# ScalarE does exponential, squares of the tile before, then the side eviction, in every step of a language-model tower

## The chip, the cores and the metric

One core of a Trainium2 chip. The metric is the device time of one execution in microseconds, lower is better. Engines: PE does matrix products, VectorE (DVE), ScalarE (ACT) and GpSimd (POOL) do elementwise work, SyncE (SP) issues transfers. Each has its own queue, worked off in order; they meet through semaphores.

## The reference

For 16 sequences of 1024 tokens, three layers are added up:

```
h = tok(x)                      # embedding, 128x128 linear, 6 gated convolutions (3 taps), 128x128 linear
h = h + attn(layernorm(h))      # 4-fold windows gate a mix of two attentions, 8 heads of width 16
h = h + ffn(layernorm(h))       # linear, experts 128 -> 512 -> 128 with gelu, linear, gelu

# in attn, for both attentions a = 1, 2 and every head:
A_a   = softmax(q_a k_a^T * scale)                       # 1024 x 1024
stats = mean, std, max, min of A_a over windows of 4 rows
alpha = sigmoid(mlp(stats of A_1 and A_2))
out   = (alpha * A_1 + (1 - alpha) * A_2) v
```

The standard deviation needs, for each row, the sum of squares of its probabilities. The kernel gets it from exp of twice the shifted score, so that a pass of ScalarE over the scores yields it as the row sum.

## The kernel before, in words

**Units and steps.** One batch is one sequence. It has 16 units (2 attentions x 8 heads), each unit 8 tiles of 128 rows by 1024 keys: 128 steps a batch, 16 batches, 2048 steps, in a loop. The stages of the same batch that come ahead of attention (tokens, convolutions, projections) and behind it (gate, output, experts) are cut into *side tasks*. A planner (`plan`) puts them into the steps ahead of time, `STEP[n]`: those behind attention for the batch before, those ahead of it for the batch after. 95 of the 128 steps have one with a product on PE.

**A step on each engine**, in queue order:

- PE: scores of tile n into one of two slots of `ps_s`; the weighted sum of values for tile n-14 into `ps_o`; the transposed scores of tile n-12 into `ps_t`, which has one slot; then the side product into `ps_w`. All share line L389, so they are told apart by what they write.
- VectorE: `row_max` (L715) copies the negated scores into one of four slots of `neg_s` and gives the row's maximum; `row_min` (L723) reads the tile before; then its side task. In step 8j+5 that is the transposition of a unit's result from `ps_o` to `o_raw` (L731), for which PE's weighted sum of the next step waits.
- ScalarE: `exp_t` (L586) of the transposed scores, from `ps_t` to `exps`; then its side task, mostly the eviction of `ps_w` (L590, L593, L655); then `squares` (L579) of tile n from `neg_s`, with the row sum.
- GpSimd: its own side tasks only: gate of a convolution, layer norms, splitting of queries and keys into bf16 parts (`qk`, which SP then loads for the next unit), splitting of row maxima (`msplit`), from which VectorE makes `mrow`.

**What sets the order.** Scores of tile n wait for the row maximum of tile n-2; transposed scores n wait for exponential n-1; the exponential waits for them. The squares wait for the row maximum of their tile and for an earlier pass of squares; the row maximum of tile n waits for the squares of tile n-4, whose slot it writes. Inside the loop `bank_of` gives the same bank, `ps_w`, to every side product, and `wait_bank` makes each wait until the reader of the one before is done:

```
at = users.index(task) - (1 if phase == "body" else 3)
if at >= 0:
    wait_side(eng, phase, i, READER[users[at][0]], users[at])
```

**Side tasks by name.** `conva`, `convg`: halves of a gated convolution (128x256 to evict); `attw`, `fc1`, `fc2`: the expert stage (`fc1` evicts two pieces of 128x256); `attT`, `nT`, `xnT`, `embT`: four transposes (128x512 to evict); `qk`: a projection of queries or keys, evicted to `stage`; `win`: window means of the statistics. `std`, `gelu1` and `gelu2` need other function tables of ScalarE, so a table load stands before and after them. In steps 64 to 79 `fc1` and convolutions take turns; in 57 to 64 `attw` and convolutions do.

Of the kernel before, what the change touches and what calls it, by code (L numbers as in the profile page):

```python
# [21 lines left out]
ACT = mybir.ActivationFunctionType  # L22
# [4 lines left out]
T = L // P  # L27
# [4 lines left out]
STEPS = U * T  # L32
# [5 lines left out]
RING = 4  # L38
SLOTS_S = 4
# [122 lines left out]
def tower_kernel(nc, ids, table, consts, w_e2h, b_e2h, conv_w, conv_b, w_h2e, b_h2e, wq1, wk1, wq2, wk2, wv, wo,  # L162
                 gw1, gb1, gw2, gb2, gw3, gb3, ln_g, ln_b, attn_w, attn_b, fc1_w, fc1_b, fc2_w, fc2_b,
                 next_w, next_b, out):
    NB = ids.shape[0] - 1

    with ExitStack() as ctx:
        def sb(name, shape, dt=F32):
            return ctx.enter_context(nc.sbuf_tensor(name, shape, dt))

        def sem(name):
            return ctx.enter_context(nc.semaphore(name))
# [32 lines left out]
        neg_s = sb("neg_s", [P, SLOTS_S, L])  # L205
        junk = sb("junk", [P, 2, L], BF16)
# [48 lines left out]
        s_max = sem("s_max")  # L255
        s_min = sem("s_min")
        s_sq = sem("s_sq")
# [14 lines left out]
        def wait_side(eng, phase, i, of, task=None):  # L272

            eng.wait_ge(side_sem[of], side.upto(phase, i, of, task))
# [112 lines left out]
        def _(pe):  # L387
# [53 lines left out]
            def task(phase, i, tk):  # L441
# [40 lines left out]
                elif kind == "attw":  # L482
# [3 lines left out]
                    for q in range(2):  # L486
                        last = mm(bank[:, P * q:P * q + P], x2[:, 2 * c + q, :], ident, start=False,
                                  skip_group_check=True)
                elif kind == "fc1":
                    _, c, j = tk  # L490
                    if (c, j) == (0, 0):
                        pe.wait_ge(s_exw, i * 64 + 64)
# [21 lines left out]
                elif kind in ("conva", "convg"):  # L514
                    _, l, c = tk
                    if l == 0:
                        w("act", ("e2h", min((CH * c + CH) // 512, 1)))
                    else:
                        w("pool", ("convg", l - 1, min(c + 1, NC - 1)))
                    g = kind == "convg"  # L520
                    for k in range(TAPS):
                        last = mm(bank[:, CH * g:CH * g + CH], cw[:, l, k, P * g:P * g + P],
                                  xc[:, l % 2, CH * c + k:CH * c + k + CH], start=(k == 0), stop=(k == TAPS - 1))
                elif kind == "h2e":
                    w("pool", ("convg", LAYERS - 1, NC // 2 * (tk[1] + 1) - 1))
                    for q in range(4):
                        t = 4 * tk[1] + q
                        last = mm(bank[:, P * q:P * q + P], xc[:, 0, 1 + P * t:1 + P * t + P], wh2e[:, :])
                elif kind == "xnT":
                    w("pool", ("ln1",))  # L530
                    last = turn(bank, xn, tk[1])
                elif kind == "qk":
                    _, a, which, k = tk
                    if a == 0:
                        w("act", ("xnT", k))
                    last = mm(bank[:, :], wqk[:, a, which, :], xn_t[:, 512 * k:512 * k + 512])
                elif kind == "v":
                    w("act", ("xnT", tk[1]))
                    for q in range(4):
                        t = 4 * tk[1] + q  # L540
                        last = mm(bank[:, P * q:P * q + P], xn_t[:, P * t:P * t + P], wv_s[:, :])
# [28 lines left out]
        def _(act):  # L570
            def squares(i, n):

                r, t = n // T % RING, n % T
                if t == 0:

                    wait_side(act, "body", i, "pool", ("unit", n // T - 2) if n // T > 1 else None)
                act.wait_ge(s_max, i * STEPS + n + 3)
                act.wait_ge(s_sq, i * STEPS + n + SLOTS_S - 1)
                nc.scalar.activation(junk[:, n % 2, :], neg_s[:, n % SLOTS_S, :], ACT.Exp, scale=-1.0,  # L579
                                     bias=negmax[:, r, t:t + 1],  # L580
                                     accum_out=sumsq[:, r, t:t + 1]).then_inc(s_sq, 1)

            def exp_t(i, n):
                act.wait_ge(s_pv, i * STEPS + n + 1)
                act.wait_ge(s_st, i * STEPS + n + 1)
                nc.scalar.activation(exps[:, n % RING, :], ps_t[:, :, :].rearrange("p c q -> p (c q)"), ACT.Exp,  # L586
                                     scale=0.5).then_inc(s_exp, 1)
# [87 lines left out]
            nc.scalar.activation(g3h[:, :], g3b[:, :], ACT.Copy, scale=0.5)  # L675
            nc.scalar.activation(cb_half[:, :], cb[:, :], ACT.Copy, scale=0.5).then_inc(s_init, 1)
            act.wait_ge(s_init, 4)
            act.sem_inc(s_sq, SLOTS_S)
            act.sem_inc(s_exp, 1)
            act.sem_inc(s_mrow, 64)  # L680
            for tk in PRE:
# [1 line left out]
            with act.Fori(0, NB // E) as group:  # L683
                for e in range(E):
                    i = group * E + e
                    for n in range(STEPS):
                        exp_t(i, n)
                        for tk in STEP[n]:
                            task("body", i, tk)
                        squares(i, n)  # L690
            for n in range(LAG_T):
                exp_t(NB, n)
            for tk in TAIL:
# [389 lines left out]
```

## Time and profile before

| | |
|---|---|
| time, median of 3 runs | 5982.09 us (5976.68 to 5983.98) |
| profiled execution | 5978.36 us, its span 5975.9 us |
| mean granted PE clock | 0.955 of full |
| busy: PE, DVE, ACT, POOL | 87%, 86%, 87%, 41% |
| instructions | 121038 |

A busy share is the time in which an engine has an instruction in work, over the span. The column "idle before, releaser" of a group says how long its engine had stood still ahead of its instructions, and whose work ended that. In the timeline, each line is one instruction or a run of like ones, with its start, its length, its engine and source line, and in brackets the idle time ahead of it.

### The profile page before, as it was taken

The page shows a single profiled execution, that of the slowest core. Times are in us where ns is not written, and L with a number is a line of the kernel's source. Part 1 is how long each engine was busy: PE and PEld are TensorE (multiplying, and loading weights), DVE is VectorE, ACT ScalarE, POOL GpSimd, SP SyncE. Part 2 cuts the span into 40 slices and gives each one's busy share as a digit, 9 for nine tenths or more (in the row PEclk, how much of TensorE's full clock was granted, in tenths as well). Part 3 has the DMA queues.
Part 4 walks back from the last instruction along what each step waited for, and adds up shares of the span by engine and source line. Part 5 has one row for each costly group of instructions (what it writes and reads, how often), then busy time and mean ns, then how long its engine had stood idle before and what let it go on. Part 6 is the DMA issues. An engine that isn't in the chain of part 4 may idle for free.

```text
span 5975.9 us, 121038 instructions
## 1 busy us (share of the span) xinstructions
PE 5203.4 (87%) x34070; PEld 2503.5 (42%) x34070; DVE 5115.8 (86%) x7715; ACT 5221.3 (87%) x7937; POOL 2454.1 (41%) x4439
## 2 busy tenths in 40 slices
PE   6988989889898988989889898988889899898985
PEld 4443434444343443434334343443434344343443
DVE  2989899898998989899898988989899898988982
ACT  2999989899898989989889898989989899898984
POOL 6525344252433525344352433525344352533423
PEclk8999999999999999999999999999999999999997
DMA  1001010010101001010010101001010010101000
GB/s 37 20 23 27 17 31 20 21 27 23 27 19 29 20 21 27 19 31 19 21 28 23 27 19 29 20 21 27 20 31 18 22 28 21 27 20 29 19 22 12
DMA packets 164933, 140.87 MB, mean 24 GB/s; under 512 B 89196, under 2 KB 108268, under 8 KB 164140
## 3 DMA queue, kind: packets, MB, share of 16 engines
q1 hardware_dynamic: 159100, 124.09, 9.0%
q0 software_dynamic: 4352, 8.92, 0.7%
q8 instruction: 291, 4.77, 0.3%
q14 instruction: 374, 3.06, 0.2%
q10 hardware_dynamic: 816, 0.02, 0.0%
HBM read 21.26 MB, written 8.91 MB: 5 GB/s over the span
## 4 chain that ended last, share of the span: by engine, by line
PE 44%; issue 18%; DVE 15%; ACT 11%; POOL 8%; SPq 1%; DMA 1%; DVEq 1%; ACTq 1%; POOLq 1%
PE ps_w L389 19%; PE ps_t L389 10%; PE ps_o L389 9%; DVE neg_s L715 7%; PE ps_s L389 6%; DVE rowmin L723 4%; ACT exps L586 3%; ACT junk L579 3%; DVE bn L735 1%; SPq L330 1%; DVE o_raw L731 1%; POOL part L866 1%; POOL ctmp L986 1%; POOL ctmp L998 1%; ACT hpre L635 1%
## 5 line engine op out<-in xcount | busy, mean ns | idle before, releaser
L715 DVE TENSOR_SCALAR_CACHE_REDUCE neg_s<-ps_s 128x1024 f32<-128x1024 f32 x2048 | 2487.5, 1215 | 599.3 <-PE ps_s L389 526.2
L723 DVE TENSOR_REDUCE rowmin<-neg_s 128x1 f32<-128x1024 f32 x2049 | 2489.5, 1215 | 0.0
L579 ACT ACTIVATE junk<-neg_s,negmax 128x1024 bf16<-128x1024 f32 x2048 | 2353.0, 1149 | 149.4 <-DVE neg_s L715 145.1
L586 ACT ACTIVATE exps<-ps_t 128x1024 f32<-128x1024 f32 x2060 | 2110.6, 1025 | 255.6 <-PE ps_t L389 252.7
L389 PE MATMUL ps_t<-qst,kst 99*128 99x512 bf16 x4120 | 1293.3, 397 | 367.5 <-ACT exps L586 364.1
L389 PE MATMUL ps_o<-exps,v_cur 128*32 128x256 f32 x16512 | 1360.8, 402 | 272.6 <-DVE o_raw L731 240.7
L389 PE MATMUL ps_s<-kst,qst 96*128 96x512 bf16 x4096 | 1260.4, 389 | 44.1 <-DMA kst<-part 35.8
L389 PE MATMUL ps_w<-xc,cw 128*128 128x256 f32 x4704 | 1185.3, 388 | 1.0
L389 PEld LDWEIGHTS ps_w<-xc,cw 128*128 128x128 f32 x4704 | 914.7, 195 | 223.3 <-ACT chan L590 8.9
L389 PEld LDWEIGHTS ps_o<-exps,v_cur 128*32 128x32 f32 x16512 | 330.1, 109 | 1198.1 <-issue 643.9
L866 POOL TENSOR_SCALAR ctmp<-ug 128x256 f32<-128x256 f32 x408 | 165.8, 406 | 1554.7 <-ACT ug L655 1533.0
L389 PEld LDWEIGHTS ps_t<-qst,kst 99*128 99x128 bf16 x4120 | 237.2, 98 | 1289.6 <-ACT exps L586 671.3
L389 PEld LDWEIGHTS ps_s<-kst,qst 96*128 96x128 bf16 x4096 | 399.6, 100 | 456.3 <-issue 162.9
L579 ACT ACTIVATION_READ_ACCUMULATOR junk<-neg_s,negmax 128x1 f32 x2048 | 407.5, 199 | 0.0
L986 POOL TENSOR_TENSOR ctmp<-ctmp,va 128x256 f32<-128x256 f32 x408 | 298.0, 730 | 33.9
L987 POOL TENSOR_TENSOR ctmp<-ctmp,xc 128x256 f32<-128x256 f32 x408 | 279.4, 685 | 32.0
L866 POOL TENSOR_SCALAR mparts<-negmax 128x8 bf16<-128x8 f32 x256 | 52.2, 204 | 580.4 <-DVE neg_s L715 540.5
L590 ACT ACTIVATE va<-ps_w,cb 128x256 f32<-128x256 f32 x392 | 185.5, 473 | 91.0 <-PE ps_w L389 77.7
L655 ACT ACTIVATE ug<-ps_w,cb_half 128x256 f32<-128x256 f32 x392 | 186.4, 475 | 64.6 <-PE ps_w L389 64.0
L866 POOL TENSOR_SCALAR xc<-ctmp 128x256 f32<-128x256 f32 x408 | 167.6, 411 | 67.6 <-POOL ctmp L987 67.6
L866 POOL TENSOR_SCALAR part<-stage 128x512 bf16<-128x512 f32 x132 | 82.1, 622 | 257.8 <-ACT stage L590 243.6
L715 DVE DVE_READ_ACCUMULATOR neg_s<-ps_s 128x1 f32 x2048 | 170.6, 83 | 0.0
(181 smaller groups left out, 4025.1 us busy)
## 6 DMA issues: line engine op xcount, KB each, us to landing
qst<-part SPq DMA_DIRECT2D x1542, 32.0 KB, 2.0
kst<-part SPq DMA_DIRECT2D x1542, 32.0 KB, 2.0
qst<-mrow SPq DMA_DIRECT2D x1028, 1.5 KB
out_dram<-z SPq DMA_DIRECT2D x17, 512.0 KB, 3.2
fc1s<-in_fc_w SPq DMA_DIRECT2D x17, 256.0 KB
fc2s<-in_fc_w SPq DMA_DIRECT2D x17, 256.0 KB
cw<-in_conv_w SPq DMA_DIRECT2D x1, 2304.0 KB
odif<-in_table,idx POOLq DMA_INDIRECT x136
```

The lines of the kernel that those rows point to most:

```text
L330: sp.dma_start(dst[HD * g:HD * g + HD, r, :], part[HD * h:HD * h + HD, a, w, c, :])\
L389: return nc.tensor.matmul(dst, lhs, rhs, start=start, stop=stop, **kw)
L579: nc.scalar.activation(junk[:, n % 2, :], neg_s[:, n % SLOTS_S, :], ACT.Exp, scale=-1.0, bias=negmax[:, r, t:t + 1], accum_out=sumsq[:, r, ...
L586: nc.scalar.activation(exps[:, n % RING, :], ps_t[:, :, :].rearrange("p c q -> p (c q)"), ACT.Exp, scale=0.5).then_inc(s_exp, 1)
L590: return nc.scalar.activation(dst, src, ACT.Identity, **kw)
L635: last = nc.scalar.activation(hpre[:, f, :], hpre[:, f, :], ACT.Gelu)
L655: last = nc.scalar.activation(ug[:, c % 2, :], bank[:, CH:2 * CH], ACT.Tanh, scale=0.5, bias=cb_half[:, 2 * l + 1:2 * l + 2])
L715: nc.vector.tensor_scalar(neg_s[:, n % SLOTS_S, :], ps_s[:, n % 2, :], -1.0, None, ALU.mult, ALU.min, accum_out=negmax[:, r, t:t + 1]).the ...
L723: nc.vector.tensor_reduce(rowmin[:, r, t:t + 1], neg_s[:, m % SLOTS_S, :], axis=AX, op=ALU.max, negate=True).then_inc(s_min, 1)
L866: return nc.gpsimd.tensor_scalar(*args)
L986: chain(i, tt(ctmp[:, 1, :], ctmp[:, 0, :], va[:, c % 2, :], ALU.mult))
L987: chain(i, tt(ctmp[:, 2, :], ctmp[:, 1, :], x_in, ALU.add))
```

## The change

In each step ScalarE does the exponential of tile n, then the squares of tile n-1 (instead of n), then its side task. The squares of the last tile of all are done behind the loop, and the first pass of the loop, for which there is no tile, runs on the zeroed buffer. The counts that are waited for are moved by one with it.

```
 def squares(i, n):
-    r, t = n // T % RING, n % T
+    m = (n - 1) % STEPS
+    r, t = m // T % RING, m % T
     if t == 0:
-        wait_side(act, "body", i, "pool", ("unit", n // T - 2) if n // T > 1 else None)
-    act.wait_ge(s_max, i * STEPS + n + 3)
-    act.wait_ge(s_sq, i * STEPS + n + SLOTS_S - 1)
-    nc.scalar.activation(junk[:, n % 2, :], neg_s[:, n % SLOTS_S, :], ACT.Exp, scale=-1.0,
+        wait_side(act, "body", i, "pool", ("unit", m // T - 2) if m // T > 1 else None)
+    act.wait_ge(s_max, i * STEPS + n + 2)
+    act.wait_ge(s_sq, i * STEPS + n + SLOTS_S - 2)
+    nc.scalar.activation(junk[:, m % 2, :], neg_s[:, m % SLOTS_S, :], ACT.Exp, scale=-1.0,
                          bias=negmax[:, r, t:t + 1],
                          accum_out=sumsq[:, r, t:t + 1]).then_inc(s_sq, 1)
...
-act.sem_inc(s_sq, SLOTS_S)
+act.sem_inc(s_sq, SLOTS_S - 1)
...
     for n in range(STEPS):
         exp_t(i, n)
+        squares(i, n)
         for tk in STEP[n]:
             task("body", i, tk)
-        squares(i, n)
+squares(NB, 0)
```

## Rows read from the trace of the kernel before

**Rows 1.** The page's busy times: engine, busy us, share of the span, instructions.
```profile
PE 5203.4 (87%) x34070; PEld 2503.5 (42%) x34070; DVE 5115.8 (86%) x7715; ACT 5221.3 (87%) x7937; POOL 2454.1 (41%) x4439
```

**Rows 2.** Groups by line: out<-in, shapes, count | busy, mean ns | idle before, releasers.
```profile
L715 DVE TENSOR_SCALAR_CACHE_REDUCE neg_s<-ps_s 128x1024 f32<-128x1024 f32 x2048 | 2487.5, 1215 | 599.3 <-PE ps_s L389 526.2
L579 ACT ACTIVATE junk<-neg_s,negmax 128x1024 bf16<-128x1024 f32 x2048 | 2353.0, 1149 | 149.4 <-DVE neg_s L715 145.1
```

**Rows 3.** Timeline of a convolution step: start us, length, engine, line, what [idle before].
```profile
3126.68 0.60 PE L389 MATMUL ps_t<-qst,kst 99*128 99x512 bf16 x2
3127.12 1.46 PE L389 MATMUL ps_w<-xc,cw 128*128 128x256 f32 x6
3127.38 1.03 ACT L586 ACTIVATE exps<-ps_t 128x1024 f32<-128x1024 f32 x1
...
3128.69 0.47 ACT L590 ACTIVATE va<-ps_w,cb 128x256 f32<-128x256 f32 x1 [0.29 <-PE ps_w L389]
...
3129.51 0.60 PE L389 MATMUL ps_t<-qst,kst 99*128 99x512 bf16 x2
```

**Rows 4.** Timeline of ScalarE in a step without a side task.
```profile
3130.22 1.02 ACT L586 ACTIVATE exps<-ps_t 128x1024 f32<-128x1024 f32 x1
...
3131.14 1.14 ACT L579 ACTIVATE junk<-neg_s,negmax 128x1024 bf16<-128x1024 f32 x1
...
3132.27 1.01 ACT L586 ACTIVATE exps<-ps_t 128x1024 f32<-128x1024 f32 x1
```

**Rows 5.** Timeline, VectorE late behind a layer norm, up to the unit's transposition.
```profile
3114.94 1.15 ACT L579 ACTIVATE junk<-neg_s,negmax 128x1024 bf16<-128x1024 f32 x1 [2.60 <-DVE neg_s L715]
...
3122.77 0.44 DVE L731 STREAM_TRANSPOSE o_raw<-ps_o 128x256 f32<-128x256 f32 x1
...
3123.26 0.64 PE L389 MATMUL ps_o<-exps,v_cur 128*32 128x256 f32 x8 [0.87 <-DVE o_raw L731]
```

**Rows 6.** Timeline of a side product that waits for the bank.
```profile
3150.52 0.78 ACT L590 ACTIVATE chan<-ps_w,col 128x512 f32<-128x512 f32 x1
...
3151.36 1.56 PE L389 MATMUL ps_w<-xc,cw 128*128 128x256 f32 x6
...
3153.86 0.60 PE L389 MATMUL ps_t<-qst,kst 99*128 99x512 bf16 x2
```

**Rows 7.** Timeline of an fc1 step, the convolution step behind it, and a unit's wait.
```profile
3175.42 0.60 PE L389 MATMUL ps_t<-qst,kst 99*128 99x512 bf16 x2
...
3177.05 0.83 ACT L590 ACTIVATE hpre<-ps_w,fc1bs 128x256 f32<-128x256 f32 x2
...
3177.83 0.61 PE L389 MATMUL ps_t<-qst,kst 99*128 99x512 bf16 x2
...
3180.67 0.60 PE L389 MATMUL ps_t<-qst,kst 99*128 99x512 bf16 x2
...
3188.22 0.64 PE L389 MATMUL ps_o<-exps,v_cur 128*32 128x256 f32 x8 [0.41 <-DVE o_raw L731]
```

**Rows 8.** Timeline of an attw step: its score product and the next.
```profile
3159.11 0.61 PE L389 MATMUL ps_t<-qst,kst 99*128 99x512 bf16 x2
...
3161.53 0.60 PE L389 MATMUL ps_t<-qst,kst 99*128 99x512 bf16 x2
```

**Rows 9.** Timeline behind ScalarE's table switches: exponential and PE's next side product.
```profile
3058.87 1.00 ACT L586 ACTIVATE exps<-ps_t 128x1024 f32<-128x1024 f32 x1
...
3060.46 1.12 PE L389 MATMUL ps_w<-cst,gin 128*64 128x32 f32 x16
...
3225.24 1.00 ACT L586 ACTIVATE exps<-ps_t 128x1024 f32<-128x1024 f32 x1
...
3227.13 2.77 PE L389 MATMUL ps_w<-xc,cw 128*128 128x256 f32 x6
```

**Rows 10.** Timeline at a batch's end: POOL behind the stage, VectorE behind POOL.
```profile
3333.44 0.62 POOL L866 TENSOR_SCALAR part<-stage 128x512 bf16<-128x512 f32 x1 [0.60 <-ACT stage L590]
...
3338.90 0.21 DVE L755 STREAM_TRANSPOSE mrow<-mparts 128x32 bf16<-128x32 bf16 x1 [1.26 <-POOL mparts L916]
```

## The prediction

> **What bounds the kernel now.** I read the busy shares first. PE, VectorE and ScalarE stand within one per cent of each other at 86 to 87% [rows 1], so none of them is the bound by its sum, and the answer lies in who waits for whom, step by step. The groups by line come second: VectorE's row maximum sat idle 599.3 us, of which 526.2 were for PE's scores, and ScalarE's squares sat idle 149.4 us, of which 145.1 were for VectorE's row maximum [rows 2]. The second number is what the new order takes away. The timeline then says whether ScalarE's wait lay on the path.
>
> A step with a convolution is PE's: from one transposed score product to the next 2.83 us (3126.68 to 3129.51), the side product starting 0.44 after the first [rows 3]. ScalarE follows: exponential 0.70 after the score product, eviction 0.29 us late because it waits for PE. A step without a side product is VectorE's (its row maximum alone takes 1215 ns, and a second pass as long follows) [rows 2]; there ScalarE runs exponential, 0.92 later squares, 1.13 later the next exponential [rows 4].
>
> ScalarE's long waits for VectorE stand where VectorE does a side job. One is 2.60 us at 3114.94; but VectorE is the late engine there, and stays so without a gap until its transposition of the unit at 3122.77, which frees PE at 3123.26 [rows 5]. PE can't pass that point, however early ScalarE had been. I find the same in each such stretch of the batch from 2997 to 3357 us: all end at a unit's transposition or at a wait for POOL. So the wait that goes was cover, not path.
>
> **The change part by part.** It adds no instruction inside the loop and one pass of squares behind it (about 1.1 us, once; the sum takes 1). Nothing is issued past SP's or POOL's queue, and ScalarE issues no DMA in the loop. What moves is the side eviction: from right behind the exponential to behind a pass of squares, that is 1.13 us later [rows 4], wherever it didn't wait for PE.
>
> Three waits get a price of nothing. The squares' own wait (row maximum of tile n-1) is met one step earlier. The row maximum now needs a pass that ScalarE does one step later; it is covered by PE, because scores(n) stand behind a score product that waits for exponential n-2, which follows those squares in ScalarE's queue. POOL's statistics wait for squares of 13 steps before. Without that cover each would cost up to the 1.13 us.
>
> The price is in the bank. Inside the loop all side products share one bank of PSUM, and each waits until the one before has been evicted. Of 128 steps 95 have a side product; in 69 pairs of neighbours the first is evicted by ScalarE. Behind the moved eviction PE's product waits as at 3151.36: it starts 0.06 us after the eviction's end (3150.52 + 0.78), and its weights, no longer loaded beside other work, make it 2.50 us to the next score product where 2.39 is usual (3127.12 to 3129.51): 0.11 more [rows 3, 6].
>
> An estimate from these rows, for an exponential that starts on time: the eviction starts 0.70 + 0.92 + 1.13 = 2.75 us after its step's score product; with duration d the next side product has started, in effect, at 2.75 + d + 0.06 + 0.11. It wanted to start at the step's length + 0.44. For a batch of 128 steps:
>
> - fc1 before a convolution, 7 pairs. d = 0.83, so 3.75; the fc1 step is 2.41 us long (3175.42 to 3177.83), so 2.85 was wanted: 0.90 late. In two of the seven PE already waits for the unit's transposition (0.41 at 3188.22), which hides that much: 5 x 0.90 + 2 x 0.49 = 5.5 us. The convolution after an fc1 gives nothing back, since PE now sets the pace: the pair was 5.25 us (to 3180.67) and becomes 6.15 [rows 7].
> - attw before a convolution, 4 pairs, one of them behind a unit's wait. d = 0.47, step 2.42 us: 3.39 against 2.86, 0.53 each [rows 3, 8], together 1.6 us.
> - Behind ScalarE's table switches. After the standard deviation (exponential at 3058.87) the product of the next step starts at 3060.46; with squares ahead of the eviction it starts at 58.87 + 0.92 + 1.13 + 0.47 + 0.06 = 61.45, 1.0 late, and 0.3 more comes in from the three convolutions before it: 1.3 us. After the Gelu (exponential at 3225.24) the same sum gives 27.82 against 27.13, with the weights 0.8 us [rows 9].
> - Transposes (d up to 0.78, steps near 2 us): nT 1.15 us; attT 1.3, all but 0.45 inside the wait for a unit; xnT 0.2. Together 1.8 us.
> - The query and key products at the end of a batch. POOL waits 0.60 us for ScalarE's stage at 3333.44, and from there its splitting of operands is one row of work up to the loads of the next batch; VectorE waits 1.26 us for the same POOL at 3338.90 [rows 10]. The stage comes 1.13 later, and so does the whole end: 1.15 us.
> - A convolution before any other product: d = 0.47 gives 3.39 against 3.27, about 0.11 in ten places, and 0.4 where a convolution follows a step without a product: 1.5 us.
>
> Other neighbours cost nothing by this sum: the fc2 steps are longer than 3.2 us, and steps 5 to 11, 43 to 46 and 50 to 53 are VectorE's, where PE has more than it loses.
>
> Sum: 5.5 + 1.6 + 1.3 + 0.8 + 1.8 + 1.15 + 1.5 = 13.65 us a batch, 16 batches 218 us, and 1 us behind the loop. The profiled execution took 5978.36 us, so 6197; it stands 3.7 us under the median of the runs, so 6201 there. I take 6200.
>
> From both sides: an eviction that PE never waits for costs nothing, and if ScalarE's waits for VectorE were path, the change gives back up to 145.1 us [rows 2]. At the other end every one of the 69 pairs loses 1.13 + 0.11 us: 69 x 1.24 x 16 = 1369 us. I stand near the first end, because a convolution step of 2.83 us covers nearly all of an eviction that ends 0.70 + 0.92 + 1.13 + 0.47 = 3.22 us after the step's score product, and most pairs begin with a convolution; only short PE steps with long evictions lose much.
>
> Two rules of the Trainium skill pull apart here. Trace row first: PE's product at 3151.36 could not start before ScalarE had emptied the one bank [rows 6]. The Trainium skill ("Perfetto Trace Analysis", section Matmuls) says that independent groups of matmuls should rotate through banks so that evictions overlap the next group; with one bank, by that rule, each later eviction shows in full, the 1369 us above. The trace agrees for that pair only: in rows 3 the overlap is there without a second bank, in the time that PE spends on the scores.
> The Trainium skill ("Perfetto Trace Analysis", section Optimization Strategy) says to find the gaps of the most contended engine and make what it waits for start sooner. ScalarE is that engine by busy share [rows 1], its gap is 145.1 us, and by this rule the kernel gains them; rows 5 speak against it.
>
> **The rivals.**
> Faster: ScalarE never stands still for VectorE, so the exponential, and with it PE's next score product, comes sooner, and PE runs ahead into the convolution steps. For it: 145.1 us of idle on the busiest engine, some 9 us a batch. Against: after each, VectorE is busy without a gap up to a unit's transposition. It decides if PE reaches a convolution stretch before such a point. All of it gives 5982 - 145 = 5837 us, half of it 5909.
> No change: PE comes to its side product later than I think, and the evictions stay hidden: 5970 to 5994 us. For it: in convolution steps ScalarE waits for PE and not the other way round. Against: fc1, where the eviction begins as soon as the exponential is over and PE's next product follows within 0.4 us of its end.
> Half: the units' transpositions take in more of the delays than the three that I counted, and about 80 us are left: 6060 us; down to 6000.
> No cover at all: 1369 us more, 7351.
>
> **How the numbers follow.** My case (6080 to 6310) 0.77; half or less 0.07; no change 0.05; faster 0.10; no cover 0.01. Taking in the small loss, 6010 to 6310 holds some 0.82. Two tenths of a per cent, 12 us, is about what a measurement of this kernel can tell from no change: faster 0.10, same 0.05, slower 0.85.
>
> **What would show it.** In the profile after, ScalarE's squares have nearly no idle for VectorE, and PE and its weight loads have a new wait for ScalarE's evictions (hpre, xa, chan), of some 10 us a batch. An fc1 and a convolution together take 6.1 us instead of 5.25; the win product starts 2.6 us after its exponential instead of 1.6; VectorE waits longer for scores than 526 us. I am wrong if the pair stays at 5.25, if the convolution steps grow by more than 0.1 us, or if the stretch from 3113 to 3123 gets shorter.

## The result, and the profile after

The changed kernel takes 6257.49 us (median of 4 runs, 6245.23 to 6265.52) beside 5980.35 us for the kernel before on the same chip (4 runs): ratio 1.0462, interval [1.0443, 1.0481], 277 us slower where 218 were forecast. The profiled executions have spans of 6243.2 and 5975.9 us, 267 us apart; the profiled one of the changed kernel is the fastest of its four.

The busy times after (engine, busy us, share of the span, instructions), to be held against [rows 1]:

```profile
PE 5340.1 (86%) x34070; PEld 2475.3 (40%) x34070; DVE 5122.2 (82%) x7715; ACT 5173.9 (83%) x7939; POOL 2445.6 (39%) x4439
```

VectorE and ScalarE do the same work in a longer span: their shares fell, so for them the time went into waits. PE's busy time rose by 137 us, that of the convolutions' products alone by 51 (1185.3 to 1236.1 us): products took longer at a lower clock, as shown below. Groups by line after (busy us, mean ns | idle before, releaser; the line numbers moved a little), to be held against [rows 2]:

```profile
L717 DVE TENSOR_SCALAR_CACHE_REDUCE neg_s<-ps_s 128x1024 f32<-128x1024 f32 x2048 | 2486.7, 1214 | 829.3 <-PE ps_s L389 728.6
L587 ACT ACTIVATE exps<-ps_t 128x1024 f32<-128x1024 f32 x2060 | 2108.9, 1024 | 876.3 <-PE ps_t L389 870.1
L580 ACT ACTIVATE junk<-neg_s,negmax 128x1024 bf16<-128x1024 f32 x2049 | 2346.9, 1145 | 9.0 <-DVE neg_s L717 9.0
```

The change did what it says: the squares' wait for VectorE fell from 145.1 to 9.0 us. But the exponential now waits 870.1 us for PE (252.7 before), and VectorE 728.6 us for PE's scores where it was 526.2. PE in turn has waits that the kernel before hardly had. The view of waits after (engine, line, waited for: us in total, times, longest):

```profile
PEld ps_w L389 <- ACT hpre L591: 71.5, 64, 1.1
PEld ps_w L389 <- ACT va L591: 65.9, 128, 1.4
PEld ps_w L389 <- ACT ug L656: 58.5, 106, 1.4
PE ps_w L389 <- ACT hpre L591: 58.2, 112, 0.7
PEld ps_w L438 <- ACT chan L594: 37.4, 31, 1.3
```

These are the weights and products of the one shared bank, standing still for ScalarE's evictions: of fc1 (hpre), of the convolutions (va, ug) and of a transpose (chan). Some of the weight loads' waiting lies beside other work of PE.

An fc1 step and the convolution behind it, after (timeline: start, length, engine, line, what [idle before]), to be held against [rows 7]:

```profile
3310.82 0.60 PE L389 MATMUL ps_t<-qst,kst 99*128 99x512 bf16 x2
...
3313.23 0.61 PE L389 MATMUL ps_t<-qst,kst 99*128 99x512 bf16 x2
...
3313.58 0.83 ACT L591 ACTIVATE hpre<-ps_w,fc1bs 128x256 f32<-128x256 f32 x2
...
3314.46 1.56 PE L389 MATMUL ps_w<-xc,cw 128*128 128x256 f32 x6 [0.62 <-ACT hpre L591]
...
3316.95 0.61 PE L389 MATMUL ps_t<-qst,kst 99*128 99x512 bf16 x2
```

The eviction starts 2.76 us after its step's score product and ends at 3314.41; the convolution starts 0.05 later, and the pair is 6.13 us long, 5.25 before. The forecast had 2.75, 0.06 and 6.15.

To see where in a batch the time went, I took the start of every exponential from the trace and the mean length of each step over batches 1 to 14. In the table, the first column of numbers is the kernel before in us, the others are what a kernel takes more (the experiments are told of below):

```
steps            before  after    lag  order  fc1,attw  no bank  conv   hold   std  defer
                                 only   only    first    of fc1  only     42  first
  5-13 qk, embT   23.50  +1.21  +0.01  +0.95   +1.33    +1.34   -0.18  +1.00  +1.14  -0.10
 17-20 conv       10.28  +0.35   0.00  +0.93   +0.35    +0.35   +0.36  +0.35  +0.35   0.00
 21-25 std, win   15.44  +2.14  +0.14  +3.47   +2.05    +2.55   +2.59  +1.40  -0.18  -0.27
 31-38 attT       21.34  +0.65   0.00  +0.65   +0.66    +0.65   +0.23  +0.70  +0.65   0.00
 41-47 ln2, conv  20.92  +1.42  +0.70  +2.47   +1.12    +1.02   +0.42  +1.75  +1.21  +0.49
 48-56 ln3, nT    24.48  +0.98  +0.01  +2.72   +0.98    +0.98   +0.01  +0.99  +0.98  -0.01
 57-64 attw       21.42  +1.80  -0.01  +1.80   +0.33    +1.80   +0.88  +1.80  +1.79   0.00
 65-79 fc1        40.43  +5.47   0.00  +5.47   +1.73    +1.21   +1.73  +5.48  +5.47   0.00
 80-84 Gelu       21.65  +1.06  +0.22  +1.59   +0.92    +1.15   +0.99  +0.95  +1.37  -1.58
 91-99 Gelu 2     27.58  +0.12  +0.01  +0.03   +0.86    +0.31   +1.02  +0.41  -0.26  -2.00
117-127 end       30.14  +1.43  -0.19  +2.76   +1.47    +1.61   +0.44  +1.55  +1.55  +0.12
a whole batch    357.39 +16.64  +0.94 +22.93  +11.86   +12.81   +9.25 +16.62 +13.95  -2.89
```

16 batches of 16.64 us are 266 us, all of the difference between the spans. Two places stand out that the forecast had not so large.

First, behind the standard deviation, after, beside [rows 9]; the second view is the timeline by windows (window, length, PE busy, PEld, DVE, ACT, POOL, granted clock, DMA share, GB/s):

```profile
3186.56 1.02 ACT L587 ACTIVATE exps<-ps_t 128x1024 f32<-128x1024 f32 x1
...
3187.64 0.60 PE L389 MATMUL ps_t<-qst,kst 99*128 99x512 bf16 x2 [1.23 <-ACT exps L587]
...
3189.21 1.11 PE L389 MATMUL ps_w<-cst,gin 128*64 128x32 f32 x16 [0.96 <-ACT va L591]
...
3192.48 2.41 PE L389 MATMUL ps_w<-xc,cw 128*128 128x256 f32 x6
```

```profile
3184.00:3187.60 3.60, 2.41 (x17) 1.25 (x15) 2.85 (x5) 3.56 (x6) 2.88 (x6) 1.00 0.00 0
3190.80:3194.60 3.80, 3.80 (x17) 2.34 (x17) 2.48 (x4) 2.13 (x4) 0.00 (x0) 0.55 0.01 2
3194.60:3200.00 5.40, 5.40 (x35) 2.54 (x34) 4.63 (x7) 3.72 (x7) 2.17 (x4) 1.00 0.12 26
```

The win product starts 2.65 us after its exponential, as forecast (1.59 before). PE waits twice, 1.23 and 0.96 us, and then comes what was not forecast: TensorE's granted clock is 0.55 in a stretch of 3.8 us, nearly all of it at the lower level of 1.2 GHz. The convolution takes 2.41 us instead of 1.46. Over the 16 batches steps 22 to 25 take 11.0 to 11.2 us in 5 and 12.6 to 14.2 in the other 11; before, 10.0 in 11 and 10.6 to 10.7 in 5.

Second, the unit's transposition of [rows 5], after:

```profile
3254.28 0.64 PE L389 MATMUL ps_o<-exps,v_cur 128*32 128x256 f32 x8 [1.83 <-DVE o_raw L733]
...
3255.29 2.22 PE L389 MATMUL ps_w<-xc,cw 128*128 128x256 f32 x6
...
3257.31 1.06 PE L389 MATMUL ps_s<-kst,qst 96*128 96x512 bf16 x2
```

```profile
3254.20:3258.20 4.00, 3.92 (x18) 2.01 (x18) 2.28 (x4) 2.51 (x4) 0.12 (x1) 0.71 0.00 0
```

ScalarE no longer waits at step 42, so PE comes earlier to the point that VectorE's transposition opens, and waits 1.83 us there instead of 0.87. Behind it the clock is at 0.71 in the mean of 4 us. PE waits the same 1.83 us in all 16 batches, but the clock does not fall in all: steps 41 to 47 take 22.5 to 22.8 us in 13 of them and 21.0 to 21.3 in 3; before, 20.9 to 21.1 in all.

### The profile page after: what moved, and what is told of

Read it like the earlier page. It is cut to its first block, busy times and chain, and to the rows that moved or that the text cites. A ratio compares the mean times of both kernels' runs of the same rounds, so it can differ in the third digit from the quotient of the medians.

```text
span 6243.2 us, 121025 instructions
## 1 busy us (share of the span) xinstructions
PE 5340.1 (86%) x34070; PEld 2475.3 (40%) x34070; DVE 5122.2 (82%) x7715; ACT 5173.9 (83%) x7939; POOL 2445.6 (39%) x4439
## 4 chain that ended last, share of the span: by engine, by line
PE 40%; issue 20%; ACT 19%; DVE 14%; POOL 5%; ACTq 1%; DVEq 1%; SPq 0%; POOLq 0%; DMA 0%
PE ps_w L389 17%; ACT junk L580 10%; PE ps_t L389 9%; PE ps_o L389 8%; DVE neg_s L717 7%; PE ps_s L389 6%; DVE rowmin L725 4%; ACT exps L587 4%; ACT hpre L591 1%; DVE bn L737 1%; DVE o_raw L733 1%; ACT hpre L636 1%; ACT L587 1%; POOL part L868 1%; POOL ctmp L1000 0%
## 5 line engine op out<-in xcount | busy, mean ns | idle before, releaser
L717 DVE TENSOR_SCALAR_CACHE_REDUCE neg_s<-ps_s 128x1024 f32<-128x1024 f32 x2048 | 2486.7, 1214 | 829.3 <-PE ps_s L389 728.6
L587 ACT ACTIVATE exps<-ps_t 128x1024 f32<-128x1024 f32 x2060 | 2108.9, 1024 | 876.3 <-PE ps_t L389 870.1
L389 PE MATMUL ps_w<-xc,cw 128*128 128x256 f32 x4704 | 1236.1, 400 | 92.6 <-ACT hpre L591 58.2
L389 PEld LDWEIGHTS ps_w<-xc,cw 128*128 128x128 f32 x4704 | 895.1, 197 | 430.5 <-ACT hpre L591 71.5
```

Source lines behind the costliest of these rows:

```text
L389: return nc.tensor.matmul(dst, lhs, rhs, start=start, stop=stop, **kw)
L717: nc.vector.tensor_scalar(neg_s[:, n % SLOTS_S, :], ps_s[:, n % 2, :], -1.0, None, ALU.mult, ALU.min, accum_out=negmax[:, r, t:t + 1]).the ...
```

## The experiments

Four runs took the change apart. **The lag alone** (e1): exponential, eviction, squares of tile n-1.

```
 exp_t(i, n)
-squares(i, n)
 for tk in STEP[n]:
     task("body", i, tk)
+squares(i, n)
```

> One half of the change alone: ScalarE does exponential n, the side eviction, then squares n-1; the eviction keeps its old place, the squares are a tile late. My theory (the loss is the late eviction, the lag is free): 5965 to 5985 us, at most 6003 if ScalarE, running ahead, lets PE's clock drop behind the unit's transposition at step 46 (1.3 us a batch). ScalarE's idle for VectorE's row maximum falls from 145 us to near 10, and the time does not follow it. Rival (the lag costs, since the row maximum waits longer for squares): over 6200. Rival (ScalarE's waits for VectorE were path): 5837 to 5909.

Measured: 5993.78 us, ratio 1.0026 [1.0016, 1.0036]. The groups of this run:

```profile
L721 DVE TENSOR_SCALAR_CACHE_REDUCE neg_s<-ps_s 128x1024 f32<-128x1024 f32 x2048 | 2487.7, 1215 | 614.0 <-PE ps_s L389 541.1
L580 ACT ACTIVATE junk<-neg_s,negmax 128x1024 bf16<-128x1024 f32 x2049 | 2354.9, 1149 | 1.5 <-DVE neg_s L721 0.9
L587 ACT ACTIVATE exps<-ps_t 128x1024 f32<-128x1024 f32 x2060 | 2114.6, 1027 | 398.6 <-PE ps_t L389 394.5
```

The squares' 145.1 us of waiting fell to 0.9, and the kernel became no faster: ScalarE stands still as long as before, only ahead of another instruction: the exponential's wait for PE grew from 252.7 to 394.5 us. VectorE's wait for scores grew by 15 us. Step 42 is 2.55 us shorter than before and steps 43 to 46 together 3.41 longer. The lag's own cost, 15.7 us, is mostly in steps 41 to 47 (+0.70 a batch): 22.5 to 22.8 us in 6 of 16 batches, as before in the others. There PE waits for the unit's transposition too, and longer than in the changed kernel:

```profile
3130.38 0.64 PE L389 MATMUL ps_o<-exps,v_cur 128*32 128x256 f32 x8 [2.01 <-DVE o_raw L737]
```

It is 2.01 or 2.02 us in all 16 batches, and the clock falls behind it in 6. Both rivals are out: that these waits were path, and that the lag itself costs over 6200.

**The order alone** (e2): exponential n, squares n, eviction; no lag.

Against the kernel before:

```
 exp_t(i, n)
+squares(i, n)
 for tk in STEP[n]:
     task("body", i, tk)
-squares(i, n)
```

> The other half alone: exponential n, squares n, then the side eviction, with no lag. My theory: the eviction is as late as in the changed kernel, and where ScalarE waits for VectorE it now holds the eviction back too, so 6257 us or more, 6260 to 6400. Rival (the lag is what costs): 5970 to 5990.

Measured: 6340.16 us, 1.0612 [1.0594, 1.0630]. fc1 and attw lose what they lose in the changed kernel (5.47 and 1.80). The lag saves 83 us once the eviction is late. In part that is because without it VectorE's lateness reaches the eviction too (steps 48 to 56: 2.72 instead of 0.98); in part the clock fell more often (steps 22 to 25 are above 13 us in 13 of 16 batches, in the changed kernel in 4).

**fc1 and attw evictions first** (e3), the rest as in the changed kernel.

```
-squares(i, n)
+first = not any(tk[0] in ("fc1", "attw") for tk in STEP[n])
+if first: squares(i, n)
 for tk in STEP[n]: task("body", i, tk)
+if not first: squares(i, n)
```

> The changed kernel, but in the steps with an fc1 or attw eviction that eviction goes ahead of the squares again. My theory: fc1 and attw were priced at 5.5 and 1.6 us a batch and measured 5.5 and 1.8, so 7.2 x 16 = 115 us come back: 6142 us, and the fc1 and convolution pair is 5.25 us long again. Rival (the loss is spread over all steps by ScalarE's order as such, and moves on to the next wait): less than 40 us come back, over 6217.

Measured: 6164.37 us, 1.0309 [1.0292, 1.0326]: 93 us came back, not 115. The convolution behind an fc1 gets its time back (3.37 to 2.50 us), but each fc1 step becomes 0.12 to 0.33 us longer. The convolution's eviction, still late, now holds up the fc1 product; in the changed kernel PE was too late itself to meet that wait. The terms don't simply add: behind the largest a smaller one had been hidden.

**fc1 without the bank** (e4): ScalarE's order and times stay as changed, but nothing waits for the late eviction.

```
+if phase == "body" and at >= 0 and users[at][0] == "fc1":
+    at -= 1                       # the next product's wait skips fc1
...
-ident_act(hpre[...], bank[...], bias=fc1bs[...])
+ident_act(hpre[...], xa[...], bias=fc1bs[...])    # inside the loop
```

> The changed kernel with ScalarE's order kept, but inside the loop the fc1 eviction reads the already evicted values in SBUF (xa) and not the bank, and the next side product waits for the eviction before it and no longer for that of fc1; this leaves out the result of fc1. My theory (the price is PE's wait for the one bank): 5.5 x 16 = 88 us come back, 6170 us, with the eviction as late as it was. Rival (the price is in ScalarE's order or in something else that waits for it): no change, 6250 to 6265.

Measured: 6185.15 us, 1.0343 [1.0326, 1.0360]: 72 us came back. The same pair of steps in this run:

```profile
3284.18 0.61 PE L391 MATMUL ps_t<-qst,kst 99*128 99x512 bf16 x2
...
3286.94 0.89 ACT L593 ACTIVATE hpre<-xa,fc1bs 128x256 f32<-128x256 f32 x2
3287.03 1.46 PE L391 MATMUL ps_w<-xc,cw 128*128 128x256 f32 x6
...
3289.43 0.60 PE L391 MATMUL ps_t<-qst,kst 99*128 99x512 bf16 x2
...
3290.28 1.13 PE L391 MATMUL ps_w<-xa,fc1s 128*128 128x256 f32 x4 [0.25 <-ACT va L593]
```

The eviction is as late as ever (2.76 us after the score product), the convolution no longer waits for it, and the pair is 5.25 us long, the value before. So the price is PE's wait for the one bank, not ScalarE's order as such. The 0.25 us in the last row is the wait for the convolution's eviction that e3 also uncovered. It stands in the steps that keep 1.21 us a batch of their loss, 19 us in all, about what the 72 us lack of 88.

**Convolutions only** (e5): squares first only in steps with a convolution.

```
-squares(i, n)
+first = any(tk[0] in ("conva", "convg") for tk in STEP[n])
+if first: squares(i, n)
 for tk in STEP[n]: task("body", i, tk)
+if not first: squares(i, n)
```

> The changed kernel, but only in the steps with a convolution do the squares go ahead of the eviction; in all others (fc1, attw, transposes, query and key products, win, Gelu) the eviction is first again. By the prediction's term for late convolution evictions, 1.5 us a batch, on top of the 5994 us that the lag alone took: 6018 us. By the fc1 steps of the run with fc1 and attw first, each 0.24 to 0.33 us longer behind a late convolution eviction, 8 a batch, some 2.1 us more: 6052 us. Rival (a late eviction costs its pass of squares, 1.13 us, wherever a product follows): some 48 convolutions, over 6500 us.

Measured: 6123.28 us, 1.0243 [1.0227, 1.0258], 130 us above the lag alone, so both of my numbers were far too low. Steps 22, 81 and 92, behind the table switches, are convolution steps as well, and I had left them out: steps 21 to 25, 80 to 84 and 91 to 99 lose 2.45, 0.77 and 1.01 us a batch over the lag alone, half of the 8.3 lost, part of it by the clock (steps 22 to 25 are above 12.5 us in 12 of 16 batches). A late convolution also costs 0.57 us in front of the first attw, and 1.73 us over the fc1 steps. The rival, 1.13 us at every convolution, is far off too: a convolution behind another, where the clock did not fall and VectorE was not late, stays between 2.84 us, which is no loss, and 3.23. Steps 5 to 13 lose nothing here, so what they lose in the changed kernel comes from other evictions. In the changed kernel products there stood still for those of the embedding's transposes (chan) and of the linear layer behind them (xc):

```profile
3144.08 0.66 PE L438 MATMUL ps_w<-cst,odif 128*128 128x128 f32 x4 [0.46 <-ACT chan L594]
...
3146.61 1.12 PE L389 MATMUL ps_w<-xn_t,wqk 128*128 128x512 f32 x2 [0.33 <-ACT chan L594]
...
3152.15 1.13 PE L389 MATMUL ps_w<-xn_t,wqk 128*128 128x512 f32 x2 [0.35 <-ACT xc L591]
```

These are steps 7, 8 and 10. Step 7 loses nothing, steps 8 and 10 lose 0.43 and 0.41.

Two runs asked about the clock. **A wait put back at step 42** (e6):

```
-act.wait_ge(s_max, i * STEPS + n + 2)
+act.wait_ge(s_max, i * STEPS + n + (3 if n == 42 else 2))
```

> The changed kernel with one wait more: at step 42 the squares of tile 41 wait until the row maximum of tile 42 is there, as the kernel before does; ScalarE then stands still some 2.5 us a batch again. My theory (what the changed kernel loses at steps 41 to 47 is TensorE's clock, which falls behind PE's longer pause at the unit's transposition in 12 of 16 batches, and PE pauses there only because it ran ahead): steps 41 to 47 come back from 22.30 to 21.0 us, about 19 us in all: 6238 us, faster by an added wait. Rival (the loss there belongs to the late evictions of the convolutions): 6257, or up to 41 us slower if the wait is path.

Measured: 6251.07 us, 1.0465 [1.0451, 1.0479]: no difference from the changed kernel. My theory failed in its second half (its 12 of 16 batches are 13 by the count above). Step 46 is whole again (2.88 us), but the fall of the clock has only moved, to step 44 and into 9 of 16 batches. One of those, step 43 and on:

```profile
3626.52 0.59 PE L389 MATMUL ps_t<-qst,kst 99*128 99x512 bf16 x2 [1.18 <-ACT exps L587]
...
3627.92 2.93 PE L389 MATMUL ps_w<-xc,cw 128*128 128x256 f32 x6 [0.81 <-ACT va L591]
```

```profile
3629.00:3633.50 4.50, 4.50 (x18) 1.94 (x17) 2.54 (x4) 1.39 (x3) 1.83 (x4) 0.50 0.09 21
```

With ScalarE held up, its late eviction makes PE wait once more, and behind the two waits the clock is at 0.50. In the 7 batches without it steps 41 to 47 take 21.3 to 21.6 us, still 0.4 above before. So neither the wait at step 42 nor the order is the cause alone.

**The eviction first in step 22 only** (e7):

```
+if n != 22:
     squares(i, n)
 for tk in STEP[n]: task("body", i, tk)
+if n == 22:
+    squares(i, n)
```

> The changed kernel, with the eviction ahead of the squares in step 22 only, the convolution before the win product. My theory: the win product starts 1.6 us behind the exponential of step 22 again, PE does not pause, and TensorE's clock does not fall behind it; steps 22 to 25 go from 12.48 to 10.3 us: 35 us in all, 6222 us. Rival (the fall of the clock belongs to the table switch and not to the pause for the eviction): only the delay of 1.1 us a batch comes back, 18 us, 6240 us.

Measured: 6202.51 us, 1.0379 [1.0364, 1.0395], 55 us under the changed kernel by the medians and 42 by the profiled spans.

```profile
3174.19 1.02 ACT L587 ACTIVATE exps<-ps_t 128x1024 f32<-128x1024 f32 x1
3175.11 0.47 ACT L591 ACTIVATE va<-ps_w,cb 128x256 f32<-128x256 f32 x1
3175.27 0.60 PE L389 MATMUL ps_t<-qst,kst 99*128 99x512 bf16 x2 [1.23 <-ACT exps L587]
...
3175.81 1.12 PE L389 MATMUL ps_w<-cst,gin 128*64 128x32 f32 x16
...
3178.41 1.46 PE L389 MATMUL ps_w<-xc,cw 128*128 128x256 f32 x6
```

PE still waits 1.23 us for the exponential, but not for the eviction, and the convolution takes 1.46 us again. Steps 22 to 25 take 10.0 to 10.2 us in all 16 batches: the clock never fell. So the second wait, for the eviction, brings the fall in this place; the table switch alone does not. (The 5 longer batches of the kernel before are another case: there the clock fell earlier, within step 21, behind a wait of PE of 1.56 us for the unit's transposition; in the changed kernel and here that wait is 1.27 us.)

Three runs used what was learnt. **Squares kept out of the way of the table switches** (e8): the kernel before, but from steps 21, 80 and 91 on the squares are one tile late, with two passes at 42, 85 and 107.

```
 for tk in STEP[n]: task("body", i, tk)
-squares(i, n)
+late = lambda m: 21 <= m <= 41 or 80 <= m <= 84 or 91 <= m <= 106
+if late(n - 1): squares(i, n - 1)
+if not late(n): squares(i, n)
```

> The kernel before (eviction ahead of squares), but at the three steps where ScalarE switches its table (21, 80, 91) it skips the squares, does them one tile late from there on, and catches up with two passes at steps 42, 85 and 107. At those three steps PE waits 0.93, 5.76 and 2.85 us for the exponential that stands behind the squares. My theory (squares are in the way only there): 0.93 + 1.14 + 1.14 = 3.2 us a batch, 51 us: 5930 us, faster than both kernels. Rival (another engine sets the end of those stretches): 5970 to 5990 us.

Measured: 5924.65 us, ratio to the kernel before 0.9909 [0.9894, 0.9925]: faster than both. Behind the Gelu the exponential now follows the table load at once (the load ends at 3197.41), beside [rows 9]:

```profile
3196.13 1.28 ACT L586 ACT_TABLE_LOAD   x1
3197.43 1.02 ACT L586 ACTIVATE exps<-ps_t 128x1024 f32<-128x1024 f32 x1
...
3198.51 0.70 PE L389 MATMUL ps_t<-qst,kst 99*128 99x512 bf16 x2 [4.64 <-ACT exps L586]
```

Steps 80 and 91 are 1.15 us shorter each, as expected; with the steps behind them that makes 1.58 and 2.00. Most of that rest is the clock: over steps 91 to 96 it is 0.91 or more in all 16 batches, 0.83 or 0.84 in 8 of them before, and over steps 80 to 84 it is 0.91 in 11 batches, at most 0.85 before. The standard deviation gains 0.27 only, where 0.93 were expected, and steps 41 to 47 lose 0.49, the clock having fallen in 10 batches. So the squares gave 2.3 us a batch, 37 of the 54 us, and it is partly luck that the sum met the 51 expected.

**Catching up at step 26** (e9), with the first range ending at 25:

```
-21 <= m <= 41
+21 <= m <= 25
```

> As the kernel that skips the squares at the three table switches, but it catches up after the first at step 26 and not at 42, so that ScalarE's order from 27 to 79 is that of the kernel before. In the run before this one steps 41 to 47 took 21.42 us on the mean and 20.88 where TensorE's clock did not fall, against 20.94 in the kernel before. My theory (the fall there comes with the late squares): 0.5 us a batch less, 8 us: 5917 us. Rival (the fall does not hang on ScalarE's order): 5921 to 5930, or slower by up to 1.13 x 16 = 18 us if step 26 has no room for a second pass.

Measured: 5928.49 us, 0.9919 [0.9906, 0.9933], no different from e8. Steps 41 to 47 came down to +0.11, but the clock still fell in 3 batches there, with the order of the kernel before; and 0.30 was lost at steps 26 to 30.

**The next exponential ahead of the Gelu** (e10), on top of that:

```
-exp_t(i, n)
+if n not in (81, 92): exp_t(i, n)
+if n in (80, 91): exp_t(i, n + 1)
```

> The last kernel, and at steps 80 and 91 ScalarE also does the exponential of the next tile ahead of the Gelu and not behind it, so that PE has one step more to do while ScalarE switches its table. ScalarE stands still 0.7 to 0.8 us for that score product first. Theory one (PE's pause behind the Gelu is path, and shrinks): 0.5 to 1 us at each of the two places, 16 to 32 us: 5885 to 5901 us. Theory two (the Gelu comes later by as much as PE gains): 5910 to 5925 us, no difference from the last kernel.

Measured: 5940.61 us, 0.9938 [0.9924, 0.9952], 12 us slower than e9, so neither theory holds for the whole. The two places differ. Behind the first Gelu steps 80 to 84 are 0.78 us a batch shorter than in e9, as theory one has it, though PE went on by one score product only and then stood at the same bank:

```profile
3203.41 2.93 PE L389 MATMUL ps_w<-xc,cw 128*128 128x256 f32 x6 [3.90 <-ACT ug L655]
```

The convolution waits 3.90 us for an eviction that stands behind the Gelu in ScalarE's queue. Behind the second Gelu steps 91 to 99 are 2.47 us longer than in e9:

```profile
3239.06 1.08 PE L389 MATMUL ps_o<-exps,v_cur 128*32 128x256 f32 x8 [2.21 <-DVE o_raw L738]
...
3240.95 1.03 PE L389 MATMUL ps_t<-qst,kst 99*128 99x512 bf16 x2 [0.81 <-ACT exps L586]
...
3241.78 2.77 PE L389 MATMUL ps_w<-xc,cw 128*128 128x256 f32 x6
```

PE, one step ahead, waits 2.21 us for VectorE's transposition of a unit, then for ScalarE, and the convolution runs at the lower clock (2.77 us instead of 1.46).

## Why the prediction was right

The mechanism was right: the eviction is the price, and the squares' wait was cover. What the sum lacked is the clock, 39 of the 266 us. By its steps, in us a batch:

- fc1: 5.5 forecast, 5.47 measured; e4 shows that it is the bank. attw 1.6, measured 1.80. Gelu 0.8, measured 1.06, about half of it the clock: steps 80 to 84 take some 22.2 us in 8 batches, at a clock of 0.85 as before (21.65 there), and 23.2 in the 8 others, at 0.78. Batch end 1.15, measured 1.43. Transposes 1.8, measured 1.4 (attT 0.43 in steps 36 to 38, nT 0.98, xnT 0.01; the rest of 31 to 38 is the convolutions').
- "The wait that goes was cover, not path" is borne out by e1. The stretch to the unit's transposition did not get shorter: steps 42 to 45, which hold the wait and the transposition of [rows 5], take 13.44 us in e1, 13.30 after and 13.03 before.
- Behind the standard deviation 1.3 were forecast, and steps 17 to 25 lose 2.49. In the batches at full clock steps 22 to 25 lose 1.05 us, which with the 0.35 of steps 17 to 20 makes 1.4; the rest of their mean loss of 2.28 (over all 16 batches), 1.2 us, is the clock.
- Too low: "steps 5 to 11, 43 to 46 and 50 to 53 are VectorE's, where PE has more than it loses". Steps 50 to 53 are so (+1.88 behind a step 49 that is 1.87 shorter). Steps 5 to 13 lose 1.21, of which 0.84 are the evictions in front of the products of steps 8 and 10; the rest was not traced. Steps 41 to 47 lose 1.42, 1.36 over all 16 batches, of which the eviction makes 0.16 (21.04 against 20.88 us in batches at full clock) and the clock 1.2. PE did have more slack there, but spent it in one pause of 1.83 us, behind which the clock fell in 13 batches. That the pause alone does it is not shown: behind the longer one of e1 it fell in 6.
- Too high: 1.5 for a convolution before another product. The steps that hold this term alone (14 to 16, 31 to 34, 95 to 103) lose 0.93. In front of fc1 it costs nothing: PE, late from the wait before, comes to that product when the eviction is over; e3 and e5 show the wait where PE is not late.

So of the 48 us between 218 and 266, the two falls of the clock make 2.4 x 16 = 39. I had priced what PE waits, not what it loses behind a wait. The other errors, up to 1.2 us a batch in either direction, leave some 10 us; that they nearly cancel is luck. The signs named beforehand came out: pair 6.13 us (6.1), win product 2.65 us (2.6), squares nearly without idle (9.0 us), and VectorE's wait for scores up. PE's weight loads alone wait some 15 us a batch for the evictions shown above, more than the 10 I named. Of the signs of being wrong, one showed in places. Outside steps 17 to 25, 41 to 53 and 80 to 84 a convolution behind another grew by at most 0.09 us, under the 0.1 named, but by 0.17 at step 34 and by 0.39 at step 99; the forecast's own 0.4 is of this kind.

The first rule weighed beforehand comes out between its two ends. The Trainium skill ("Perfetto Trace Analysis", section Matmuls) wants independent products in rotating banks so that evictions overlap. Taking fc1 alone off the bank gave back 72 us of 277 (e4), where the rule applied in full would have made the loss 1369. The other rule weighed is of the Trainium skill ("Perfetto Trace Analysis", section Optimization Strategy): find the gaps of the most contended engine and make what it waits for start sooner. It found no gain here: e1 took 144 us of ScalarE's gaps away in one place, 142 came back in another, and the kernel was 15.7 us slower.

## What to carry to other kernels

An eviction that frees a shared bank belongs ahead of work that nobody waits for soon, and the cost of delaying it is read from the consumer: only where the next product comes sooner than the eviction ends does it show. A wait of the busiest engine is worth removing only if the chain behind it does not end at another engine's gate; here 144 us of idle bought nothing, while 1.15 us of squares taken from in front of an exponential that PE had long waited for came back in full at each of the two Gelu switches, 37 of the 54 us of e8. Price a new pause of PE by what it does to the clock behind it as well.

## What the runs showed of the hardware

TensorE's granted clock fell from 2.4 to 1.2 GHz behind pairs of short waits of PE (1.23 and 0.96 us; 1.18 and 0.81 us; 2.21 and 0.81 us) and behind single ones of 1.83 us, in some batches and not in others of the same execution, though the waits at one place were nearly the same in all of them. Their length alone does not decide it: in steps 41 to 47 the clock fell in 13 of 16 batches behind 1.83 us (after) and in 6 of 16 behind 2.02 us (the lag alone). A fall there cost 0.8 us in e8, 1.5 to 1.7 after and in e1, and 2.5 to 2.9 in e6. What decides it from batch to batch stays open: e6 and e9 moved it or made it rarer, and did not end it. Only e7, which took the second wait away, did so in its place, from 11 batches to none.
